# Gated-attention scores and gate matmuls: from plain float32 operands to three float32r products of high and low parts

## The reference

```python
qp = q @ Wq + bq            # q = output of the first layer, (16, 256, 256)
kp = k @ Wk + bk            # k = v = ctx, (16, 77, 256)
vp = v @ Wv + bv
w = softmax(einsum('bqd,bkd->bqk', qp, kp) * scale)
x = einsum('bqk,bkd->bqd', w, vp)
gate = concatenate((qp, x), -1) @ Wg + bg
return x * mask[..., None] * sigmoid(gate) + q0
```

## Time and profile before

| | |
|---|---|
| median of three runs | 817.04 us (816.86 to 822.85) |
| profiled execution, device time | 817.04 us |
| its span, first to last instruction | 814.6 us |
| mean granted TensorE clock | 0.982 |
| PE busy | 763.9 us (94%), 7072 matmuls |
| PEld busy | 624.1 us (77%) |
| DVE busy | 552.6 us (68%) |
| ACT busy | 517.7 us (64%) |
| POOL busy | 461.8 us (57%) |
| chain that ended last | PE 69%, DVE 13%, issue 4%, ACT 4% |

### The profile page before, as it was taken

The page is one execution under the profiler, slowest core; times in us unless marked ns, Lnnn a source line. Parts: engine busy times, 40 slices in busy tenths (PEclk is TensorE's granted clock), DMA queues, the critical chain, the costliest instruction groups (busy, mean ns, idle before and its releaser), DMA issues.

```text
span 814.6 us, 19616 instructions
## 1 busy us (share of the span) xinstructions
PE 763.9 (94%) x7072; PEld 624.1 (77%) x7072; DVE 552.6 (68%) x1221; ACT 517.7 (64%) x1224; POOL 461.8 (57%) x582
## 2 busy tenths in 40 slices
PE   6998999999999998878798999999999999999986
PEld 5786778788877775555467988888988888988864
DVE  4435787878788988877878666686668554663453
ACT  4532465656565566556677888888777887855542
POOL 2413477776767676564346566656555588556330
PEclk9999999999999999899779999999999999999999
DMA  9686686888577674355332222222220100011132
GB/s 285 162 260 185 147 144 116 160 138 138 108 125 129 104 114 101 82 117 104 67 74 58 38 57 57 54 55 57 55 47 7 46 2 6 26 57 51 50 95 81
DMA packets 105305, 76.49 MB, mean 94 GB/s; under 512 B 43262, under 2 KB 101968, under 8 KB 104948
## 3 DMA queue, kind: packets, MB, share of 16 engines
q1 hardware_dynamic: 101850, 72.36, 41.7%
q10 hardware_dynamic: 3360, 2.90, 1.2%
HBM read 25.49 MB, written 11.42 MB: 45 GB/s over the span
## 4 chain that ended last, share of the span: by engine, by line
PE 69%; DVE 13%; issue 4%; ACT 4%; DMA 1%; POOL 0%; ACTq 0%; DVEq 0%
PE a_misc L89 13%; PE a_s L1035 10%; PE a_pair L89 10%; PE a_s L800 4%; PE a_pair L824 4%; PE a_s L798 3%; PE a_pair L842 3%; PE a_pair L996 3%; PE a_pair L1122 3%; PE a_pair L981 3%; PE a_pair L1134 3%; DVE a_nm L1476 2%; PE a_s L958 2%; DVE c_z L1586 2%; PE a_s L1093 2%
## 5 line engine op out<-in xcount | busy, mean ns | idle before, releaser
L1201 ACT ACTIVATE a_pT<-a_pair 128x512 f32<-128x512 f32 x192 | 113.7, 597 | 79.9 <-PE a_pair L824 72.6
L1975 POOL TENSOR_TENSOR c_hidden<-c_hid,c_hidden 128x256 fp32r<-128x256 f32 x128 | 94.8, 741 | 122.1 <-ACT c_hidden L1365 122.0
L1476 DVE TENSOR_REDUCE a_nm<-a_s 128x2 f32<-128x512 f32 (+1 forms) x192 | 126.9, 677 | 44.8 <-PE a_s L800 44.2
L1035 PE MATMUL a_s<-c_w,c_hidden 128*128 128x256 f32 x768 | 118.4, 293 | 0.0
L1331 ACT ACTIVATE a_pT<-a_pair 77x512 f32<-77x512 f32 x128 | 75.4, 589 | 66.4 <-PE a_pair L981 65.3
L1882 POOL TENSOR_SCALAR_AFFINE_SELECT a_pT<-a_pT 128x256 f32<-128x256 f32 (+1 forms) x192 | 90.9, 492 | 21.9 <-ACT a_pT L1201 21.4
L89 PE MATMUL a_pair<-c_fxh,c_w 128*128 128x256 f32 x512 | 99.9, 288 | 1.0 <-ACT c_hid L1357 1.0
L1035 PEld LDWEIGHTS a_s<-c_w,c_hidden 128*128 128x128 f32 x768 | 99.1, 190 | 0.8 <-issue 0.4
L1651 DVE TENSOR_REDUCE a_nm<-a_s 128x5 f32<-128x385 f32 (+1 forms) x96 | 55.4, 577 | 51.6 <-PE a_s L958 51.3
L89 PEld LDWEIGHTS a_pair<-c_fxh,c_w 128*128 128x128 f32 x512 | 79.3, 191 | 1.2 <-ACT c_hid L1357 1.2
L824 PE MATMUL a_pair<-a_sq,a_sk 98*128 98x256 bf16 (+1 forms) x512 | 75.1, 250 | 3.7 <-ACT a_pT L1201 2.8
(11 more groups left out here) (259 smaller groups left out, 2003.5 us busy)
## 6 DMA issues: line engine op xcount, KB each, us to landing
a_sq<-a_parts SPq DMA_DIRECT2D x96, 128.0 KB, 4.3
a_sk<-a_parts SPq DMA_DIRECT2D x96, 128.0 KB, 4.3
a_sq<-c_parts SPq DMA_DIRECT2D x96, 128.0 KB
x<-in_xT SPq DMA_DIRECT2D x16, 256.0 KB, 5.2
res<-in_x SPq DMA_DIRECT2D x16, 256.0 KB, 5.3
out<-g_fin SPq DMA_DIRECT2D x16, 256.0 KB, 2.1
a_sk<-kc_parts SPq DMA_DIRECT2D x96, 38.5 KB
g_vv<-vv_rows SPq DMA_DIRECT2D x16, 154.0 KB
```

Source lines behind the costliest of these rows:

```text
L1035: last = mt(down[:, qt * D:(qt + 1) * D], (hh, hl)[x](m)[:, qt * P:(qt + 1) * P], w2(y, m), start=m == 0 and qt == 0 and i == 0, stop=m == ...
L1201: nc.scalar.activation(pT[g % NPT][:], stps[g % 2][:], ACT.Exp).then_inc(s_exp, 1)
L1476: nc.vector.tensor_reduce(nm[c % 2][:, QT * heads[0] + qt:QT * heads[-1] + qt + 1:QT], sps[g % 2][:].rearrange("p (h k) -> p h k", h=len(h ...
L1975: nc.gpsimd.tensor_tensor(hl(m), hid[n % NHID][:], f32(hh(m)), ALU.subtract).then_inc(c_hl, 1)
```

## The change

In `context_products` the eviction of `fold` becomes two steps: ACT writes the high part (semaphore `s_ah`), and a new DVE instruction writes the low part from the same PSUM tile (`s_al`); PE's waits for the tile are now on `s_al`. On DVE the six new instructions stand where `remainder(1)` stood, and `remainder(1)` stands after the fourth of them. `wqg` gets a low part on DVE as well. `fold` and `wqg` are twice as large in SBUF, in DRAM and in the transfers, whose number stays.

In the GATED stage `gx` becomes `gxh` (ACT, the same instruction as before) and `gxl` (DVE, new, `gated_x_low(e+1)`, ahead of `shares(e)`), and both products use `mm3`. Everyone who waited for `gx` now waits for `gxl`.

```diff
-            remainder(1)
+            for n in range(KT * NC):
+                ot, c = divmod(n, NC)
+                c0, cn = CCH[c]
+                dve.wait_ge(s_ah, n + 1)
+                nc.vector.scalar_tensor_tensor(fold[:, c0 // SC:(c0 + cn) // SC, 1, ot, 0:SC], byb(kps[n % 2], 0, cn), colv[:, ot:ot + 1],
+                                               f32(fold[:, c0 // SC:(c0 + cn) // SC, 0, ot, 0:SC]), ALU.add, ALU.subtract).then_inc(s_al, 1)
+                if n == NC:
+                    remainder(1)
...
+            dve.wait_ge(s_wqgh, 1)
+            nc.vector.tensor_tensor(wqg[:, 1, :, :], two(fps[0]), f32(wqg[:, 0, :, :]), ALU.subtract).then_inc(s_wqgl, 1)
...
-                atleast(pe, s_fold, n - 1)
+                atleast(pe, s_al, n - 1)
...
                 if c < 2:
-                    pe.wait_ge(s_fold, KT * NC - 1 + c)
+                    pe.wait_ge(s_al, KT * NC - 1 + c)
...
-                    act.wait_ge(s_fold, KT * NC)
+                    act.wait_ge(s_al, KT * NC)
...
-                pe.wait_ge(g_x, c + 1)
+                pe.wait_ge(g_xl, c + 1)
...
-                    for kt in range(KT):
-                        mt(o, gx[c % 3][:, kt, qt * P:(qt + 1) * P], fold[c % ND][:, kt, :], start=kt == 0, stop=False)
+                    mm3(nc.tensor, o, lambda x, kt: (gxh, gxl)[x][c % 3][:, kt, qt * P:(qt + 1) * P], lambda y, kt: fold[c % ND][:, y, kt, :],
+                        range(KT), stop=False)
                     last = mt(o, one[:], cb[c % ND][:], start=False, stop=True)
...
-                    for kt in range(KT):
-                        last = mt(xo(c)[:, qt * 2 * D + D:(qt + 1) * 2 * D], gx[c % 3][:, kt, qt * P:(qt + 1) * P], wqg[:, kt, :],
-                                  start=kt == 0, stop=kt == KT - 1)
+                    last = mm3(nc.tensor, xo(c)[:, qt * 2 * D + D:(qt + 1) * 2 * D], lambda x, kt: (gxh, gxl)[x][c % 3][:, kt, qt * P:(qt + 1) * P],
+                               lambda y, kt: wqg[:, y, kt, :], range(KT))
...
+            def gated_x_low(c):
+                if not real(c):
+                    return
+                dve.wait_ge(g_xh, c + 1)
+                nc.vector.tensor_tensor(gxl[c % 3][:], two(turned_rows(c)), f32(gxh[c % 3][:]), ALU.subtract).then_inc(g_xl, 1)
...
                 if k == 3:
+                    gated_x_low(e + 1)
                     shares(e)
```

More of the change, by code:

```diff
@@ L134, in context_products @@
     wkq = [sb(f"wkq{i}", [P, KT, D], F32R) for i in range(2)]
-    wqg = sb("wqg", [P, KT, D], F32)
+    wqg = sb("wqg", [P, 2, KT, D], F32R)
     parts = nc.alloc_sbuf_tensor_at("x_parts", [P, 3, B, KT, SC], BF16, offset=t.place["a_sq1"])
     rest = [sb(f"rest{i}", [P, 512], F32) for i in range(2)]
-    fold = sb("fold", [P, B, KT, SCE], F32)
+    fold = sb("fold", [P, B, 2, KT, SCE], F32R)
     NRING = len(t.value_stored)
@@ L206, in _ @@
             sp.dma_start(d.cb, f32(cb[:].rearrange("o b x s -> o (b x s)"))).then_inc(cb_stored, 16)
-            sp.wait_ge(s_wqgc, 1)
-            sp.dma_start(d.wqg, wqg[:].rearrange("p k c -> p (k c)")).then_inc(g_stored, 16)
+            sp.wait_ge(s_wqgl, 1)
+            sp.dma_start(d.wqg, f32(wqg[:].rearrange("p x k c -> p (x k c)"))).then_inc(g_stored, 16)
             for i in range(NTOK):
@@ L378, in _ @@
                 act.wait_ge(s_a, n + 1)
-                nc.scalar.activation(fold[:, c0 // SC:(c0 + cn) // SC, ot, 0:SC], byb(kps[n % 2], 0, cn), ACT.Identity,
-                                     bias=colv[:, ot:ot + 1]).then_inc(s_fold, 1)
+                nc.scalar.activation(fold[:, c0 // SC:(c0 + cn) // SC, 0, ot, 0:SC], byb(kps[n % 2], 0, cn), ACT.Identity,
+                                     bias=colv[:, ot:ot + 1]).then_inc(s_ah, 1)
                 if n == NC:
@@ L387, in _ @@
             act.wait_ge(s_wqg, 1)
-            nc.scalar.activation(wqg[:], two(fps[0]), ACT.Copy).then_inc(s_wqgc, 1)
+            nc.scalar.activation(wqg[:, 0, :, :], two(fps[0]), ACT.Copy).then_inc(s_wqgh, 1)
             for i in range(NTOK):
@@ L400, in _ @@
                 if i == 1:
-                    act.wait_ge(s_fold, KT * NC)
+                    act.wait_ge(s_al, KT * NC)
                     act.wait_ge(s_pads, 1)
-                    act.dma_start(d.fold.rearrange("p b x -> p (b x)"), fold[:].rearrange("p b k s -> p (b k s)")).then_inc(a_stored, 16)
+                    act.dma_start(d.fold.rearrange("p b x -> p (b x)"), f32(fold[:].rearrange("p b x k s -> p (b x k s)"))).then_inc(a_stored, 16)
         @block.vector
@@ L466, in _ @@
         def _(pool):
-            nc.gpsimd.memset(fold[:, :, :, SC:SCE], 0.0).then_inc(s_pads, 1)
+            nc.gpsimd.memset(f32(fold[:, :, :, :, SC:SCE]), 0.0).then_inc(s_pads, 1)
             nc.gpsimd.memset(t.ident[:], 0.0).then_inc(const_zeroed, 1)
@@ L580, in causal_cross_feed_gated @@
     gvv = [gat(f"vv{i}", [SCE, 2 * D], F32, *p) for i, p in enumerate((("a_sq0", 0), ("a_sq0", half), ("a_sq1", 0)))]
-    wqg = gat("wqg", [P, KT, D], F32, "a_sq1", half)
-    gx = [gat(f"x{i}", [P, KT, S], F32, *p) for i, p in enumerate((("a_sq2", 0), ("a_sq2", 2 * quarter), ("a_sq3", 0)))]
+    wqg = gat("wqg", [P, 2, KT, D], F32R, "a_sq1", half)
+    gxh = [gat(f"xh{i}", [P, KT, S], F32R, *p) for i, p in enumerate((("a_sq2", 0), ("a_sq2", 2 * quarter), ("a_sq3", 0)))]
+    gxl = [gat(f"xl{i}", [P, KT, S], F32R, *p) for i, p in enumerate((("a_sq2", quarter), ("a_sq2", 3 * quarter), ("a_sq3", quarter)))]
     gate = [gat(f"gate{i}", [P, QT, D], F32, "a_sq3", (2 + i) * quarter) for i in range(2)]
     gz = [gat(f"z{i}", [P, QT, D], F32, "a_sk0", i * quarter) for i in range(2)]
-    fold = [gat(f"fold{i}", [P, KT, SCE], F32, "a_sk1", i * 8 * KT * SCE) for i in range(ND)]
+    fold = [gat(f"fold{i}", [P, 2, KT, SCE], F32R, "a_sk1", i * 8 * KT * SCE) for i in range(ND)]
     gated = [gat(f"gated{i}", [P, QT, D], F32, "a_sk2", i * quarter) for i in range(2)]
@@ L624, in causal_cross_feed_gated @@
     stored = [sem("out_stored") for _ in range(2)]
-    names = ("nmr", "half", "onef", "one", "pad", "z", "zg", "h", "ht", "x", "sc", "max", "exp", "rec", "p", "pt", "pth",
+    names = ("nmr", "half", "onef", "one", "pad", "z", "zg", "h", "ht", "xh", "xl", "sc", "max", "exp", "rec", "p", "pt", "pth",
              "gates", "xo", "fact", "gated", "fin", "zero", "blank")
-    (g_nmr, g_half, g_onef, g_one, g_pad, g_z, g_zg, g_h, g_ht, g_x, g_sc, g_max, g_exp, g_rec, g_p, g_pt, g_pth,
+    (g_nmr, g_half, g_onef, g_one, g_pad, g_z, g_zg, g_h, g_ht, g_xh, g_xl, g_sc, g_max, g_exp, g_rec, g_p, g_pt, g_pth,
      g_gates, g_xo, g_fact, g_gated, g_fin, g_zero, g_blank) = (sem("g_" + n) for n in names)
@@ L760, in load_gated @@
                     sp.wait_ge(g_sc, c - ND + 1)
-                sp.dma_start(fold[c % ND][:].rearrange("p k s -> p (k s)"), d.fold[:, c]).then_inc(g_fold[c % ND], 16)
+                sp.dma_start(f32(fold[c % ND][:].rearrange("p x k s -> p (x k s)")), d.fold[:, c]).then_inc(g_fold[c % ND], 16)
                 if c == 0:
@@ L775, in _ @@
                 sp.dma_start(gvv[c][SC:SCE], d.row).then_inc(g_row, 16)
-            sp.dma_start(wqg[:].rearrange("p k c -> p (k c)"), d.wqg).then_inc(g_wqg, 16)
+            sp.dma_start(f32(wqg[:].rearrange("p x k c -> p (x k c)")), d.wqg).then_inc(g_wqg, 16)
             for c in range(B):
@@ L1415, in gated_x @@
                 atleast(act, g_gates, c - 2)
-                nc.scalar.activation(gx[c % 3][:], two(turned_rows(c)), ACT.Copy).then_inc(g_x, 1)
+                nc.scalar.activation(gxh[c % 3][:], two(turned_rows(c)), ACT.Copy).then_inc(g_xh, 1)
             def gated_exps(c):
@@ L2080, in program @@
         d.vc = nc.dram_tensor("vc_rows", (CT, D), F32).ap()
-        d.fold = nc.dram_tensor("fold_rows", (P, B, KT * SCE), F32).ap()
+        d.fold = nc.dram_tensor("fold_rows", (P, B, 2 * KT * SCE), F32).ap()
         d.vv = nc.dram_tensor("vv_rows", (CT, 2 * D), F32).ap()
-        d.wqg = nc.dram_tensor("gate_weights", (P, KT * D), F32).ap()
+        d.wqg = nc.dram_tensor("wqg_parts", (P, 2 * KT * D), F32).ap()
         d.row = nc.dram_tensor("bias_row", (1, 2 * D), F32).ap()
```

20 lines of the change are left out of this document (10 added, 10 removed).

## The result

The changed kernel is slower by about 1.2%: 828.41 us (median of 8 runs, 823.81 to 830.24) against 820.13 us of before in the same session (8 runs, 815.44 to 822.85), ratio 1.0115, 95% interval 1.0093 to 1.0139. Run again later it came out at 1.0129 (1.0096 to 1.0162). The forecast was 823.9, +0.85%, with a range of 819.5 to 828.6. By the two ratios the loss is 9.4 to 10.6 us, where 6.9 was forecast.

A forecast was written before the change was run, and what follows sets the result against it. PE was taken to bound 672 to 770 us, DVE the window 772.7 to 780.5. 817.04 + 3.8 (PE's products) + 1.1 (DVE at the residual) + 2.0 (preparation) = 823.9 us, +0.85%; range 819.5 to 828.6.

The forecast's parts named there:

- What bounds the kernel: From 672 to 770 us PE is busy 97 of 98 us and sets the time; DVE, 50.5, has room.
- Gates: Gate product in a gated slot: twelve float32r matmuls at 0.12, 1.44 us for 1.73, −0.29 us for an example.
- Preparation: `context_products`: PE waits for the low part of `fold` in three gaps, 0.7, 0.3 and 1.3 us; shift +2.0 us.
- The larger store: `fold_rows` store on ACT's queue, 1248 to 2496 KB: may take three times as long before the barrier waits for it.
- The scores: Score product in a gated slot: twelve float32r matmuls of 78 columns at 0.12 us, +0.54 us for an example.
- VectorE at the residual: Near 773 us, the low part on DVE delays the last example's moments, deviation and `gate_x`: +1.1 us.
- The signs: Wrong if float32r distance isn't 0.11 to 0.125, PE idles for DVE between 672 and 770, or the barrier doesn't move.
- One sum among the rivals: Rival: weight load doesn't bound, 78-column matmuls go at 0.044 us, kernel faster at 811.5 us; chance 0.04.
- the sign turns at 0.10 us a matmul: In the faster rival, float32r score matmuls from 0.10 us down, with both low bounds together, turn the sign; chance 0.04.
- the 3.1 us of the rest: Terms outside PE's products: 1.1 us on DVE at the last feed residual and 2.0 us in the preparation.
- the loads run three examples ahead: nothing.: GATED stage: the larger loads cost nothing, with DMA share 0.14 and loads three examples ahead.
- Slow stream: Rival, scores: 78-column float32r matmuls cost 0.14 us, +0.84 each; 8.3 and 3.1 give 828.4 us; chance 0.13.

The follow-up runs named there:

- e2: Changed kernel without VectorE's sixteen low parts of the turned rows, all three products reading the high part: ratio 1.0128 to before.
- e15: The kernel before, unchanged, one more profiled execution: 43.5 us from last feed residual to end.
- e6: Kernel before with three spare VectorE fills ahead of `g_gated` of chunk 9, to lengthen TensorE's pause: ratio 1.0029 to before.
- e9: The changed kernel run again, unchanged: ratio 1.0129 to before.
- e3: Changed kernel with one float32 product per pair, of the high parts, in scores and gates; preparation, transfers and low part kept: ratio 1.0040 to before.
- e4: Changed kernel with only the high part of `fold` made, stored and loaded; all three products read it: ratio 1.0070 to before.
- e8: Kernel before with only the gates as three float32r products, row parts made by GpSimd, scores in plain float32: ratio 0.9976 to before.
- e10: Changed kernel with VectorE doing two gated slots' work ahead of and between the last chunk's moments and deviation: ratio 1.0055 to before.
- e13: Changed kernel with two gated slots moved earlier in VectorE's order and SyncE's loads issued one chunk sooner: ratio 1.0000 to before.
- e11: Kernel before with VectorE doing two gated slots' work ahead of and between the last chunk's moments and deviation: ratio 0.9947.
- e14: Kernel before with two gated slots moved earlier in VectorE's order and SyncE's loads issued one chunk sooner: ratio 0.9950.
- e1: Changed kernel with twenty spare matmuls in TensorE's two pauses at the last feed residual: 824.5 us, ratio 1.0070 to before.
- e5: Kernel before with nine spare matmuls in TensorE's pause ahead of the gates of chunk 10: ratio 0.9980 to before.
- e16: Kernel before with only gates split (parts by GpSimd), two gated slots earlier in VectorE's order, loads one chunk sooner: ratio 0.9924 to before.
- e12: Kernel before with only gates split (parts by GpSimd) and two gated slots moved earlier in VectorE's order: ratio 0.9963 to before.
- e7: Changed kernel with SyncE's loads issued one chunk sooner, ahead of the store: ratio 1.0109 to before.

## Why the prediction missed

Right:

- **What bounds the kernel**: PE between 672 and 770 us. The effect of the products shows there, 2.3 us, and VectorE's low parts cost nothing beside it (e2: 324.77 us with them left out, 324.72 in after).
- **Gates**: 1.44 us for 1.73, as forecast.
- **Preparation**: three gaps, of 0.59, 0.22 and 1.16 us where 0.7, 0.3 and 1.3 stood, all from the low part of `fold`, the last one through the remainder that waits for `part_one`. Forecast +2.0. From PE's first product of `fold` to the first key-bias product it is 9.98 or 9.99 us in all ten traces without the split (28.60 to 38.58 in before), and 12.23 to 12.27 in all eight with it (27.32 to 39.56 in after): +2.3. The first of these products itself begins anywhere from 26.9 to 29.4 us. So the barrier in the first pair of traces moved by only 1.0 (72.91 to 73.91), which alone would have misled.
- **The larger store** of `fold` took 10.1 us for 7.2 and cost nothing that any row shows.

Wrong in size:

- **The scores**: 0.12 us for a float32r matmul of 78 columns, measured 0.11. The Trainium skill, "TensorE: Matmul & The Clock Gate", section "Back-to-back issue gap", has load and matmul set the spacing together; the 0.11 of 78 columns beside 0.12 of 256 agrees. The low side was right: +0.46 for a slot, not +0.54, so the products are +0.17 a slot and 15 x 0.17 = 2.5 us, not 3.8.
- **VectorE at the residual**, "Sum: +1.1 us". From the residual's start to the gates: 7.76 us before (772.73 to 780.49), 8.15 after (779.77 to 787.92), +0.4. The reciprocal was nearly as late as I had it, 0.98 us (0.99 after the residual before, 1.97 after). But of the small operations of the deviation, 128x2 each, one took 1.11 us in before's trace and 0.16 in after's, and another 0.83 and 1.20; the step took them for fixed. This is no chance: e15, e6 and e2, without the low part, have before's times within 0.01 us, and e9, e3 and e4, with it, after's. e2 goes from the residual to the gates in 7.76 us again, so the low part costs 0.4 us here. Where the long ones come from shows beside GpSimd's rows:

```profile
775.11 1.26 POOL L1998 TENSOR_TENSOR g_z<-g_z,ln_g 128x512 f32<-128x512 f32 x1 [5.23 <-ACT g_z L1406]
775.57 0.83 DVE L2022 TENSOR_SCALAR var<-mv 128x2 f32<-128x2 f32 x1
776.45 1.28 POOL L2004 TENSOR_TENSOR res<-g_z,ln_b 128x512 f32<-128x512 f32 x1
776.63 1.11 DVE L2026 SCALAR_TENSOR_TENSOR prod<-root 128x2 f32<-128x2 f32 x1
...
783.49 1.26 POOL L2020 TENSOR_TENSOR res<-g_z,ln_b 128x512 f32<-128x512 f32 x1
783.58 1.20 DVE L2038 TENSOR_SCALAR var<-mv 128x2 f32<-128x2 f32 x1
```

The first four are before's, the last two after's. Each long one begins while a 128x512 operation of GpSimd runs and ends within 0.04 us of its end; e8 has three of the kind (0.93, 1.19 and 1.12 us). In after these small operations come 1 us later and meet only the second of GpSimd's two, not both, which takes back 0.6 of the 1 us. No run here tests this.

The signs held. The distance of the float32r matmuls was 0.11, PE had no wait for VectorE between 672 and 770 us, and the barrier moved. None of them looks at what follows the residual. One sum among the rivals was off: the sign turns at 0.10 us a matmul for the products alone; with the 3.1 us of the rest it takes 0.085 or so (14 x 0.085 − 0.09 = 1.10, +0.07, and 15 x (0.07 − 0.29) = −3.3).

Wrong in kind, and the steps that failed:

- **"the loads run three examples ahead: nothing."** Buffers for three chunks don't mean loads three chunks ahead. The queue issues the load behind the store of the chunk just finished, so it has 3 us, for twice the data (156 KB of `fold` for 78). Its price: with VectorE's order changed, e10 to e13 saves 3.1 us of the tail, and e11 to e14 saves 1.3 on before's loads, so the change's own share is 1.8 us. With VectorE's order as it was, most of this hides behind the wait for `g_gated`: e4, whose loads have before's size, has a tail of 48.1 for 48.8.
- **No term for the clock.** I read 1.00 in the earlier trace rows and carried it over, and took PE's 2.1 idle us there as cover that costs nothing. The row was sound, but it stood over 5.69 of 7.8 us, and the change made that place emptier: before's 2.09 us of pause became two pauses of 1.04 and 1.31. The order change takes 6.1 us off after's tail and 1.3 off before's; the difference, 4.7 us, is the price of pause and fall together that the change brings. This is the largest part of what the forecast lacks.

So the tail's 6.9 us (48.8 − 41.9) part into 4.7, 1.8 and 0.4 (e13 over e14). They add up because each is a difference of tails along the same row of kernels, and another order of the steps would part them otherwise, as e4 shows. With 2.3 for preparation and 2.3 for the earlier products it is 11.5 against before's first trace, 9.9 against e15 (tail 43.5); measured were 9.4 (0.0115 x 820) and 10.6 (0.0129 x 820).

Of the rivals none was this one. "Slow stream" gives 828.4, next to the measured median, by another mechanism; a time that fits is no proof of its cause.

The fall goes with the pause ahead of the gates. Eight traces have at most 0.23 us of it (e1, e5, e10 to e14, e16), and in none of them does the clock fall there; e12's falls later, after its third wait at the scores. Of the ten traces with 1.31 us or more nine have a fall.

What stays open: what decides whether the clock falls after a pause, and for how long. In these traces, six have a shorter pause (0.29 to 1.04 us) 3.5 to 5 us ahead of the one at the gates, and all six fell for 10 to 13.7 us (after twice, e2, e3, e4, e8). With the one pause alone, four traces had three outcomes: none (2.09 us, before), 3.4 us (1.99, e15; 3.65, e6) and 10 us (2.60, e7). Three pauses of 0.55 to 0.98 us, 6 us apart, brought none (e10), and three of 0.31, 0.50 and 1.48 us brought 3.4 us (e12). That is a pattern and no test of it. Nor was the cause of the spread between 330 and 424 us tried, where the clock also falls in every trace.

## What to carry to other kernels

Where TensorE pauses near the end of a chain on another engine, price the pause as well as what it can set off: here two pauses of 2.35 us in all were followed by a clock at half speed for 13.7 us, where one of 2.09 was followed by none. Look at what stands between the last producer and the one result that TensorE waits for: moving 4.7 us of small VectorE work behind it took 0.5% off the kernel before (0.9947) and 0.7% off the changed one (1.0129 to 1.0055). And count how far ahead a load is issued from the queue's own timeline; the number of buffers tells only how far it could be.
